# A gated recurrence unrolled over all groups with two sequences on the partition halves, and a cosine attention with its norms and first scores between the q and v projections

## The reference, cut to what matters

```
q = silu(xn Wq); z = xn Wk + delta; k = sigmoid(-z); v = xn Wv
S_t = exp(logsigmoid(z_t)) * S_(t-1) + k_t v_t ; o_t = q_t S_t   (per head)
o = rmsnorm_per_head(o * sigmoid(xn G1 G2)) * norm_w;  x = x + o Wo
```

## Time and profile before

| | before |
|---|---|
| three runs | 6859.3, 6864.2, 6873.4 us (median 6864.2) |
| the profiled execution | 6861.8 us |
| its span in the trace | 6859.7 us |
| mean granted clock of TensorE | 0.94 of full speed |
| busy: PE, DVE, ACT, POOL | 89%, 64%, 51%, 32% of the span |

### The profile page before, as it was taken

The page is one execution under the profiler, slowest core; times in us unless marked ns, Lnnn a source line. Parts: engine busy times, 40 slices in busy tenths (PEclk is TensorE's granted clock), DMA queues, the critical chain, the costliest instruction groups (busy, mean ns, idle before and its releaser), DMA issues. The chain is left out here.

```text
span 6859.7 us, 128543 instructions
## 1 busy us (share of the span) xinstructions
PE 6081.4 (89%) x50945; PEld 3477.3 (51%) x50945; DVE 4362.3 (64%) x7548; ACT 3526.7 (51%) x5768; POOL 2191.8 (32%) x1461
## 2 busy tenths in 40 slices
PE   7999987999877777998658999999999999999998
PEld 4666664444432223676434555555555555555554
DVE  3444443444348886333447888888888888888885
ACT  3434433666434443443425666666666666666664
POOL 0000000222214443000005555555555555555553
PEclk9999987999968888999769999999999999999999
DMA  1000000222200000000001111111111111111111
GB/s 52 1 1 1 1 1 13 50 50 49 61 8 0 0 1 0 1 0 0 0 22 35 32 41 41 32 38 42 35 37 43 36 34 45 36 32 46 39 37 26
DMA packets 183558, 174.97 MB, mean 26 GB/s; under 512 B 24021, under 2 KB 174070, under 8 KB 182774
## 3 DMA queue, kind: packets, MB, share of 16 engines
q1 hardware_dynamic: 182998, 167.18, 10.2%
HBM read 30.79 MB, written 2.10 MB: 5 GB/s over the span
## 5 line engine op out<-in xcount | busy, mean ns | idle before, releaser
L2367 POOL TENSOR_TENSOR local_ssum<-local_sq 128x512 f32<-128x512 f32 x384 | 696.3, 1813 | 2298.0 <-ACT local_sq L2155 2297.8
L2375 POOL TENSOR_TENSOR local_rot<-local_rot,local_inv_all 128x512 f32<-128x512 f32 x768 | 964.3, 1287 | 92.8 <-DMA local_inv_all<-local_inv 92.5
L1976 PE MATMUL banks<-local_y,local_Wqkv 128*128 128x512 f32 x1536 | 824.5, 619 | 63.9 <-ACT local_sq L2155 61.0
L861 POOL TENSOR_TENSOR cosine_summed<-cosine_probs 128x512 f32<-128x512 f32 x128 | 172.6, 1349 | 1678.6 <-ACT cosine_probs L750 1678.5
L2177 ACT ACTIVATE local_probs<-local_probs,local_npeak 128x1152 f32<-128x1152 f32 x384 | 482.7, 1257 | 355.2 <-DVE local_probs L2281 355.2
L2281 DVE TENSOR_TENSOR local_probs<-banks,band 128x576 f32<-128x576 f32 x768 | 546.2, 753 | 184.2 <-PE banks L2011 178.9
L2261 DVE TENSOR_TENSOR local_rot<-banks,local_rotary_scaled 128x512 f32<-128x512 f32 x768 | 525.6, 684 | 193.5 <-PE banks L1976 188.2
L2155 ACT ACTIVATE local_sq<-banks 128x512 f32<-128x512 f32 x768 | 459.4, 598 | 253.8 <-DVE local_sin L2262 244.1
L2268 DVE TENSOR_TENSOR local_rot<-local_rot,local_sin 128x1024 f32<-128x1024 f32 x384 | 512.3, 1334 | 41.2 <-DVE local_sin L2262 1.4
L2171 ACT COPY local_v<-banks 128x512 f32<-128x512 f32 x384 | 224.8, 586 | 595.0 <-PE banks L1989 594.5
L2011 PEld LDWEIGHTS banks<-local_rot 32*128 32x128 f32 x12288 | 415.5, 185 | 225.1 <-issue 202.4
(11 more groups left out here) (401 smaller groups left out, 10884.5 us busy)
## 6 DMA issues: line engine op xcount, KB each, us to landing
local_inv_all<-local_inv SPq DMA_DIRECT2D x768, 128.0 KB, 2.7
cosine_inv_all<-cosine_inv SPq DMA_DIRECT2D x256, 128.0 KB, 2.7
local_Wqkv<-in_L_ffn_Wqkv_quads SPq DMA_DIRECT2D x36, 256.0 KB, 2.8
local_Wo<-in_L_ffn_Wo_quads SPq DMA_DIRECT2D x6, 512.0 KB, 4.1
experts_w_W<-in_L_ffn_W SPq DMA_DIRECT2D x1, 2048.0 KB
out<-x SPq DMA_DIRECT2D x8, 256.0 KB, 2.3
local_W<-in_L_ffn_W SPq DMA_DIRECT2D x12, 170.5 KB, 2.4
cosine_w_Wqkv<-in_L_attn_w_kv SPq DMA_DIRECT2D x1, 1024.0 KB
```

The lines of the kernel that those rows point to most:

```text
L1976: pe.matmul(seqs(banks[:, QK_BANK, :]), Wqkv[:, at:at + P], y_group(g), start=True, stop=True).then_inc(qk_projected, 1)
L2367: pool.tensor_tensor(ssum[:, n % 2, m, :], sq[:, 0, :], sq[:, 1, :], ALU.add).then_inc(square_summed, 1)
L2375: pool.tensor_tensor(a, a, twice(inv_all[:, n % 2, m, of_seq(s)]), ALU.mult).then_inc(united, 1)
```

## The change

In the gated recurrence the two sequences of a group lie on the two partition halves: sequence 0 on partitions 0 to 63, sequence 1 on 64 to 127. The same data become 128 partitions by 512 elements, and each of them fits one PSUM bank instead of two. The stage is written out for all groups in one block. Its semaphores count over the whole stage and it has one barrier, at its end. Step i prepares group m = i, works on g = i-1, ends e = i-2, and takes the LayerNorm of group i+1 ahead. The keys are turned by a product with the identity in place of the transpose operation. The number of products and the number of columns in each stay the same, except that the output is turned by 4 transposes of 128 columns in place of 8 of 64. A constant `causal_chunks` (128x64) is loaded at the start.

```diff
-        sgate_of, vals_of = sb("sgate", [CHUNK, 2, NC, D]), sb("vals", [CHUNK, 2, NC, D])
-        att = sb("att", [CHUNK, HEADS, NC, CHUNK])
+        sgate, vals = sb("sgate", [P, 2, SC, D]), sb("vals", [P, 2, SC, D])
+        att = sb("att", [P, HEADS, SC, CHUNK])
...
-            restart(nc, sems)
-        pipeline(nc, step)
+        chunks = [(b, i, b * SC + i) for i in range(SC) for b in range(GB)]
...
+                def turn_keys(g):
+                    for b, i, c in chunks:
+                        last = pe.matmul(banks[side(b), KEY_BANKS, wide(i)], k[:, g % 2, ch(c)], consts["ident"], start=True, stop=True)
+                    last.then_inc(keys_turned, 1)
```

More of the change, by code:

```diff
@@ L687, in _ @@
                         norm(n)
+                    if (n := within(i - 2)) is not None:
+                        score(n, 0)
                     if within(i) is not None:
@@ L847, in _ @@
                         clamp(n)
+                    if (n := within(i - 4)) is not None:
+                        normalize(n)
                     if within(i) is not None:
@@ L1546, in gated_recurrence @@
+        ms, lms, rms = (sb(n, [P, SC * HEADS]) for n in ("ms", "lms", "rms"))
         oT = sb("oT", [P, GN])
[L1547 to L1552, removed]
@@ new lines, in normalize_x, with take_projections @@
+                def normalize_x(m):
+                    dve.wait_ge(rstd_done, m + 1)
+                    if m:
+                        dve.wait_ge(turned, m)
+                    for t in range(GT):
+                        dve.tensor_scalar(xn[:, t, :], tiles(m)[:, t, :], moments[:, t, 0:1], rstd[:, t:t + 1],
+                                          ALU.subtract, ALU.mult).then_inc(normed, 1)
+                def take_projections(m):
+                    dve.wait_ge(z_projected, m + 1)
+                    if m == 0:
+                        dve.wait_ge(w["loaded"], w["total"])
+                    if m:
+                        dve.wait_ge(k_sigmoid, m)
+                    dve.tensor_scalar(z[:], banks[:, VALUE_BANK, :], w["delta"][:], None, ALU.add).then_inc(z_biased, 1)
+                    dve.wait_ge(low_projected, m + 1)
+                    if m:
+                        dve.wait_ge(gates, m)
+                    dve.tensor_copy(low[:], banks[0:HW, GATE_BANK, :]).then_inc(low_copied, 1)
@@ new lines, in normalize_out, with add_out @@
+                def normalize_out(g):
+                    dve.wait_ge(rms_ready, g + 1)
+                    oh = o[:].rearrange("p c (h d) -> p (c h) d", d=HW)
+                    dve.tensor_tensor(oh, oh, spread(rms[:], HW), ALU.mult).then_inc(o_normed, 1)
+                def add_out(g):
+                    dve.wait_ge(out_ready, g + 1)
+                    dve.tensor_tensor(tiles(g), tiles(g), banks[:, END_BANK, :].rearrange("p (t d) -> p t d", d=D), ALU.add).then_inc(added, 1)
+                for i in range(-1, GROUPS + 2):
+                    m, g, e, ahead = within(i), within(i - 1), within(i - 2), within(i + 1)
+                    if ahead is not None:
+                        measure(ahead)
+                    if m is not None:
+                        take_projections(m)
+                    if e is not None:
+                        mean_square(e)
+                    if g is not None:
+                        mask(g)
+                    if m is not None:
+                        decays(m)
+                        take_values(m)
+                    if e is not None:
+                        normalize_out(e)
+                    if g is not None:
+                        states(g)
+                    if ahead is not None:
+                        normalize_x(ahead)
+                    if e is not None:
+                        add_out(e)
+                    if m is not None:
+                        decayed(m)
+                    if g is not None:
+                        gate(g)
@@ L1790 @@
+        restart(nc, [*norms, *made, *worked, *ended])
 QUADS = H // 4
```

477 lines of the change are left out of this document (259 added, 218 removed).

## The result

The changed kernel takes 6668.6 us (median of 4 runs, 6660.0 to 6673.7), against 6863.7 for the kernel before on the same chip: ratio 0.9712, 95% interval 0.9700 to 0.9724. That is 195 us less where 160 less was forecast (6704 us). A few single executions of the later runs took far longer (8853 us and more); every ratio goes by the others. The profiled run took 6673.7 us.

The account below looks back on a forecast made before the run. Engine-to-engine waits and a barrier bound the recurrence, PE the cosine attention. From 6861.8 us, 141 (recurrence) and 20 (cosine) less, 0.5 more for a load, gave 6701; the runs' median lies 2.4 above: 6704, range 6665 to 6748.

Parts of the forecast that it names:

- Four sets at 4.2 us: Recurrence, PE: keys, values, gates and outer products, 64 records at 0.066 us, take 4.2 us a step (bounds 4.2 and 7.8).
- attend 2.0: Recurrence, PE: the attend products of 64 columns stay at 0.062 us a record, 2.0 us a step (bounds 1.0 and 2.0).
- outputs 3.7: Recurrence, PE: output products take 3.7 us a step, including 6 changes of shape at 0.15 each; at most 5.3.
- The step at 18.0: Recurrence: following the new orders from ACT's copy of xn, one full step at full clock lasts 18.0 us, low end 16.7.
- DVE waits 9.3 to 11.2 for `outer`: Recurrence: within a step DVE waits from 9.3 to 11.2 us for PE's outer products before it starts the states.
- Rival 1, PE at the lower level: Recurrence: PE stays at its lower clock, steps take 20.5 to 22 us, stage 190, total 6732 us; chance 0.17.
- Rival 4, a ring of waits: Recurrence: three groups in flight wait on each other, nothing overlaps, a step takes 41 us, total about 6875; chance 0.02.
- The stage at 162: The whole recurrence, with six full steps of 18 us, takes 162 us in place of 302.8, 141 less.
- rival 3: Recurrence and cosine stage both go better: steps at 16.7 us, cosine gain 40, total 6668 us; chance 0.13.
- The cosine stage: -20 forecast: Cosine attention: q taken earlier gives 15 us, fewer clock drops 5, so 20 us less; ends 0 and 45.
- Of 8 steps in a group: one 0.85, two 0.6, the others 0 or -0.15: Cosine attention: the us by which q is taken earlier in each step; 1.9 us a group, 15 us in 8 groups.
- Rival 2: Cosine attention: v's copy behind the exponentials stalls PE in each of 64 steps, +19 us instead of -20, total 6743; chance 0.14.

Follow-up runs that it names:

- the kernel with the filled gap: The changed kernel with three unread 256-column products on PE in its wait before turning the recurrence's output; ratio 0.9707 to the kernel before.
- the meeting: The changed kernel with the recurrence cut into one block per step, so all engines meet between steps; ratio 0.9741 to the kernel before.

## Why the prediction came out as it did

**The method held.** PE's sets of products at full clock can be read off the kernel with the filled gap, start to start:

```profile
3273.80 0.69 PE L1614 MATMUL banks<-hgrn_q,hgrn_k 64*64 64x64 f32 x32
3274.43 1.09 PE L1622 MATMUL banks<-ident,hgrn_k 128*64 128x128 f32 x16
3275.35 1.04 PE L1595 MATMUL banks<-hgrn_w_Wv,hgrn_xnT 128*64 128x128 f32 x16
...
3279.00 1.16 PE L1629 MATMUL banks<-hgrn_vals,hgrn_keys 64*128 64x128 f32 x16
3280.09 1.09 PE L1601 MATMUL banks<-hgrn_w_G,hgrn_low 64*64 64x128 f32 x16
3281.11 1.16 PE L1660 MATMUL banks<-hgrn_w_Wo,hgrn_oT 128*128 128x128 f32 x8
3282.20 0.45 PE L1646 MATMUL banks<-hgrn_vals,hgrn_att 64*64 64x64 f32 x8
3282.58 0.44 PE L1642 MATMUL banks<-hgrn_S,hgrn_q 128*64 128x128 f32 x4
...
3284.92 0.63 PE L1575 MATMUL banks<-ident,hgrn_xn 128*128 128x128 f32 x4
```

- *DVE 14.0 and ACT 11.8 us a step*: right, 13.4 to 13.7 and 11.7.
- *Four sets at 4.2 us*: right, 0.92 + 0.98 + 1.09 + 1.02 = 4.0. The rule of two column halves that I set beside them fits three of the four: the outer products have 64 rows and 128 outputs, and alternate the row halves. They took half, too. Transposes 0.6 each and `project_out` 1.1 lie within what I gave.
- *attend 2.0*: the term mis-sized most. It takes 0.63, 0.020 us a record and not 0.062. I took 0.062 "for they show that price already with alternating row halves". Two things were wrong with it. The earlier trace rows had them right behind the barrier, at a granted clock of 0.50, and all on one column half. The second weighs more. At the same clock of 0.50 the changed kernel's `attend` takes 1.13 us (in the run with the end in the step), so the halves give 1.97 to 1.13 and the clock 1.13 to 0.69; and at full clock with neighbours on the same half it takes 1.54. My lower bound was 1.0; even that was too high. Nor does the low end of 16.7 follow from it: in my walk DVE isn't free before 4.3, so the masks come 0.9 earlier and the walk ends at 17.2.

```profile
3375.59 1.13 PE L1614 MATMUL banks<-hgrn_q,hgrn_k 64*64 64x64 f32 x32
```

- *outputs 3.7*: 2.7. By the price of `attend` the 32 small records cost 0.6, the 12 of 128 columns at 0.0575 (line 1622) 0.7; that leaves 1.4 for 6 changes of shape, about 0.23 each against my 0.15. This split is worked out, not measured by itself. PE in all: 12.8 against 15.4.
- *The step at 18.0*: 15.7 at full clock. Laid beside the changed kernel's step that starts when xn is copied at 3258.43, with my walk in brackets: z read by 2.3 us (2.75), masks done by 4.7 (5.9), the output normalised by 7.7 (9.3), the states by 12.5 (14.2), the gate by 15.9 (18.1). Of the 2.2 us, 0.5 are there when z is read, as DVE's gate ends only 0.2 behind ACT's copy and not 0.6; 0.8 more are `attend`; the other 0.9 come bit by bit, since DVE's instructions of 128x512 start 0.60 us apart and I had given each its listed 0.68 and more:

```profile
3272.49 0.68 DVE L1810 TENSOR_TENSOR hgrn_k<-hgrn_k,hgrn_enG 128x512 f32<-128x512 f32 x1
3273.09 0.68 DVE L1813 TENSOR_TENSOR hgrn_q<-hgrn_q,hgrn_eG 128x512 f32<-128x512 f32 x1
3273.69 0.68 DVE L1845 TENSOR_TENSOR hgrn_o<-banks,hgrn_sgate 128x512 f32<-128x512 f32 x1
```

- *DVE waits 9.3 to 11.2 for `outer`*: right, 13.6 us in 7 times, 1.9 each. That this wait sets the step isn't borne out: without it (outer ahead) the step is no shorter, as DVE then waits for z and for ACT's silu, though at a clock that falls in every step. The prediction had DVE's and ACT's rounds agree "within 1 us", and that part stood.
- *Rival 1, PE at the lower level*: half true. Not the whole stage runs there, but among its full steps the clock falls three times, 2.7 us each. What I held against it, gaps of only 2 to 3 us in 18, was not enough: behind gaps of 2.02 the clock fell twice in six, behind 1.39 once in six, behind 0.53 never. The Trainium skill ("TensorE: Matmul & The Clock Gate", Part 1) led me to expect the full clock in a fuller step; the trace agrees in the two steps at 1.00 and not in the two at 0.81.
- *Rival 4, a ring of waits*: false, no step is a sum of the engines' work.
- *The stage at 162*: 154.8. The two errors had opposite signs: steps at full clock 2.3 us shorter than forecast, and 2.7 more for each fall of the clock. So the nearness to rival 3 (steps of 16.7) is in part luck.

**The cosine stage: -20 forecast, -33 in the trace, -37 in the run of that part alone.** The mechanism was right: the gap closes ahead of the v projection and opens again ahead of the k projection, on the copy of v. From taking q to `values` I counted 4.99 before and 5.0 after; the traces show 4.98 and 4.93. Five drops of the clock, in as many groups, are gone; where one fell into the count to `values`, it was 6.6 in place of 4.98, so 1.6 us each. In the stage as a whole PE's busy time fell by only 1.4 us, as the clock rose later at its start in this trace (about 1167 against 1159) and was low for longer near its end. The step that failed is "Of 8 steps in a group: one 0.85, two 0.6, the others 0 or -0.15", the times by which q is taken earlier. From the start of the q projection to the taking of q, the eight steps of a group read

```
before  3.37  2.02  1.52  1.16  1.16  1.16  1.16  3.27
after   2.77  1.16  1.06  1.16  1.16  1.16  1.16  1.70
```

The first gives 0.60 and the second 0.86, as I said. The third gives 0.46, where I had nothing, but pays it back behind (5.47 to `values`). The last gives 1.57, where I had 0.6: there the unit vectors, the statistics and the normalising all stand ahead of q, and the first of them has become shorter. Before and after, in that step:

```profile
1486.67 2.40 DVE L822 TENSOR_TENSOR cosine_qk<-cosine_qk,cosine_inv_all 128x512 f32<-128x512 f32 x2 [2.09 <-DMA cosine_inv_all<-cosine_inv]
```
```profile
1466.53 1.63 DVE L821 TENSOR_TENSOR cosine_qk<-cosine_qk,cosine_inv_all 128x512 f32<-128x512 f32 x2 [0.84 <-DMA cosine_inv_all<-cosine_inv]
```

Before, `unite` and POOL's sum of the probabilities began together (1486.67 and 1486.66); the new order of the exponentials starts that sum earlier (1465.72, 0.8 ahead of `unite`), and `unite` meets only its end. DVE's instruction falls from a mean of 1026 to 790 ns and POOL's from 1349 to 1271. I had named this contention, and only as a risk. PE's and ACT's orders alone bring the gain (800 ns), DVE's alone doesn't (1040), and with v copied first, which moves the exponentials back, it is lost again (996). Rival 2 (the copy of v late in each step) came true in its mechanism, 20.3 us, and was already in my sum.

What stays open: whether a shorter ACT chain (one table load fewer) together with `outer` first would bring the step down to DVE's 13.4. That wasn't tried, nor were the table load already saved and the keys' product with the identity undone. The parts undone one at a time (in the mean of the full steps: DVE's instructions 4.6 us, the late end 4.7, the meeting 2.9, the halves of the array 0.8, each with its part of the clock) don't add up to the 18.4 us; the rest, which I would give to the projections of the next group running beside this one's chain and to PE at full clock, was not isolated.

## What to carry to other kernels

Before a product's price is taken from a trace, read at which clock level and in which neighbourhood it stood: `attend` was priced threefold because its row had all products on one column half and lay behind a barrier, at the lower level. When a step's length comes from several engines' rounds that agree within 1 us, taking one wait away may give nothing. DVE's work as it was before (43 us) and the end of a group back in its own step (36 us) cost most of all that the experiments undid. When an edit makes a step longer, compare steps at equal clock before naming a price: most of what the meeting cost was the clock. Here the lower clock behind a gap of 2.02 us cost 2.7 us, more than the gap itself. Filling it took 7.7 us from the stage in the trace, which the whole kernel's times (4 us less) can't tell from none.

## What the hardware showed that I had not expected

- Products of 64 rows, 64 outputs and 64 columns, spread over both row and both column halves, take 0.020 us each at full clock, a third of 0.062 on one column half at the lower level. At that lower level the spread ones take 0.035 (1.13 us for 32), and at full clock with neighbours on the same half 0.048 (1.54).
- More work kept the clock: with 1.5 us of unread products per step none of the three falls came, and the stage was 7.7 us shorter.
- Of the two multiplies of 128x512 in a `unite` that begins together with POOL's sum, one takes 1.76 to 1.80 us and the other 0.69; without the sum beside them both take 0.69. POOL's sum takes 1.81 in some of these cases (1497.6) and its usual 1.27 in others (1486.7).
